# A transposed input made by VectorE from a second, blocked load, in a macaron transformer block

## The reference

```python
x = x + 0.5 * ffn(layernorm(x))        # w = int4-quantised kernel; x @ w + bias + (x @ a) @ b
x = x + attention(layernorm(x))        # 16 heads of 64, keys and values from a latent of 32 columns, causal softmax
x = x + 0.5 * ffn(layernorm(x))        # the same weights again
```

## Time and profile before

| what | value |
|---|---|
| median of 3 executions | 784.86 us (783.91 to 785.38) |
| the profiled execution | 786.69 us, of which the span of instructions is 785.0 us |
| busy: PE, PE weight loads | 757.9 us (97%), 584.5 us (74%) |
| busy: DVE, POOL, ACT | 646.7 us (82%), 648.2 us (83%), 503.2 us (64%) |
| granted TensorE clock, mean | 0.986 |
| DMA | 79.94 MB, 78,933 packets; 15,905 of them under 512 B |

### The profile page before, as it was taken

The page is one execution under the profiler, slowest core; times in us unless marked ns, Lnnn a source line. Parts: engine busy times, 40 slices in busy tenths (PEclk is TensorE's granted clock), DMA queues, the critical chain, the costliest instruction groups (busy, mean ns, idle before and its releaser), DMA issues.

```text
span 785.0 us, 20588 instructions
## 1 busy us (share of the span) xinstructions
PE 757.9 (97%) x7578; PEld 584.5 (74%) x7578; DVE 646.7 (82%) x2044; ACT 503.2 (64%) x979; POOL 648.2 (83%) x449
## 2 busy tenths in 40 slices
PE   8799999999999999999999999999999999999997
PEld 6586677778687777778777877868778776867675
DVE  3788788898889889898988989888888988777635
ACT  6158676667667576666757666675766676665670
POOL 5535778889898888979888898988888897979882
PEclk8799999999999999999999999999999999999999
DMA  4547172644636163553616254362526445260101
GB/s 118 140 101 175 30 175 57 139 109 91 159 75 140 48 144 92 115 134 83 162 42 140 72 133 117 83 166 58 133 59 146 104 98 137 63 159 3 30 2 41
DMA packets 78933, 79.94 MB, mean 102 GB/s; under 512 B 15905, under 2 KB 66353, under 8 KB 78833
## 3 DMA queue, kind: packets, MB, share of 16 engines
q1 hardware_dynamic: 78272, 77.43, 42.5%
q10 hardware_dynamic: 560, 1.20, 0.6%
HBM read 9.91 MB, written 8.39 MB: 23 GB/s over the span
## 4 chain that ended last, share of the span: by engine, by line
PE 84%; DVE 5%; ACT 3%; SPq 3%; issue 2%; DMA 1%; POOL 1%; ACTq 0%; DVEq 0%; POOLq 0%
PE bank L960 17%; PE bank L996 16%; PE bank L924 13%; PE bank L920 8%; PE bank L933 8%; PE bank L1085 7%; PE bank L1040 3%; SPq L420 3%; PE bank L1041 2%; PE bank L1042 2%; PE bank L1031 2%; PE bank L1028 2%; PE bank L1101 1%; DMA q_stack<-max_t 1%; ACT q_stack L725 1%
## 5 line engine op out<-in xcount | busy, mean ns | idle before, releaser
L1246 DVE TENSOR_REDUCE strip_max<-bank 128x8 f32<-128x512 f32 (+1 forms) x384 | 250.3, 683 | 18.5 <-PE bank L996 15.8
L756 ACT ACTIVATE later_probs<-bank 128x512 f32<-128x512 f32 x384 | 217.7, 598 | 56.0 <-PE bank L924 33.4
L621 POOL TENSOR_TENSOR totals<-totals,later_probs 128x1024 f32<-128x1024 f32 x124 | 227.4, 1834 | 12.1 <-POOL totals L621 0.4
L621 POOL TENSOR_TENSOR totals<-first_probs,later_probs 128x1536 f32<-128x1536 f32 x62 | 216.1, 3486 | 13.8 <-ACT later_probs L756 13.8
L756 ACT ACTIVATE first_probs<-bank 128x384 f32<-128x384 f32 (+1 forms) x320 | 153.6, 512 | 109.8 <-PE bank L924 69.3
L996 PE MATMUL bank<-keys,q_stack 118*128 118x512 f32 (+7 forms) x1024 | 208.1, 305 | 1.9 <-DMA q_stack<-q_high 1.1
L996 PEld LDWEIGHTS bank<-keys,q_stack 118*128 118x128 f32 x1024 | 170.2, 190 | 12.7 <-DMA q_stack<-q_high 1.3
L924 PE MATMUL bank<-q_stack,keys 119*128 119x384 f32 (+1 forms) x448 | 176.8, 412 | 1.7 <-ACT first_probs L756 1.0
L1246 DVE TENSOR_REDUCE maxima<-bank 128x1 f32<-128x512 f32 (+1 forms) x192 | 127.6, 679 | 2.6 <-PE bank L996 2.5
L924 PEld LDWEIGHTS bank<-q_stack,keys 119*128 119x128 f32 x448 | 80.8, 188 | 41.7 <-ACT later_probs L756 18.3
L920 PE MATMUL bank<-q_stack,keys 119*128 119x256 f32 x512 | 106.7, 300 | 1.4 <-DMA q_stack<-max_t 0.8
(11 more groups left out here) (152 smaller groups left out, 915.4 us busy)
## 6 DMA issues: line engine op xcount, KB each, us to landing
q_stack<-q_high SPq DMA_DIRECT2D x252, 128.0 KB, 2.4
q_stack<-q_low SPq DMA_DIRECT2D x128, 128.0 KB, 2.4
x_in<-in_L_attn_x_bld_dram SPq DMA_DIRECT2D x16, 256.0 KB, 3.4
out_dram<-x SPq DMA_DIRECT2D x16, 256.0 KB, 3.5
x_back<-out_dram SPq DMA_DIRECT2D x16, 256.0 KB, 3.2
out_dram<-x2b SPq DMA_DIRECT2D x15, 256.0 KB, 2.3
keys<-keys_staged SPq DMA_DIRECT2D x16, 192.0 KB, 2.9
keys<-keys_staged SPq DMA_DIRECT2D x32, 96.0 KB, 2.6
```

The lines of the kernel that those rows point to most:

```text
L621: nc.gpsimd.tensor_tensor(total, first_probs[g % 2][:, :, P:] if j == 1 else total, probs_of(g, j)[:], ALU.add).then_inc(added, 1)
L756: nc.scalar.activation(out, score_bank(t, u)[:, 0:heads * cols].rearrange("p (e q) -> p e q", e=heads), ACT.Exp).then_inc(exp_done, 1)
L1246: nc.vector.tensor_reduce(out, bank[:].rearrange("q (b k) -> q b k", k=strip), AX.X, ALU.max).then_inc(a_free, 1)
```

## The change

The input gets a second way in. `blocks` is a new SBUF tile of 128 partitions by 16 by 32: for each quarter `a` of the partitions, one DMA brings columns `32a` to `32a+31` of all 512 positions, position `32r+q` going to partition `32a+q`, block `r`. One VectorE transpose of 128x512, which turns each 32x32 block by itself, makes `x_t` of it. The transposes of `x_in` on PE (unit 0) and the ACT copy fall away in every round but -2, where they stay under new names (`first_transposes`, `first_copy`). The front has seven units, so all counts on `f_full` and `f_free` drop by one. SP issues the four new DMAs for batch `t+4` behind the maxima of the first half; DVE turns batch `t+3` at place 30 of round `t`. POOL's bias addition to `x_in` waits for the load instead of for unit 0. `wkv4` moves into a tile that is free at the start. The tables of places are new throughout.

```diff
-F_UNITS = 8
+F_UNITS = 7
-KEYS_UNIT, QUERY_UNIT = 3, 4
+KEYS_UNIT, QUERY_UNIT = 2, 3
-FRONT_AT = [2, 4, 11, 15, 19, 30, 31, 37]
+FRONT_AT = [4, 11, 15, 19, 29, 32, 37]
-WEIGH_AT = [[9, 9, 13, 13], [17, 21, 21, 21], [31, 31, 33, 33], [47, 47, 50, 50]]
-ONES_AT = [21, 39, 50, 50]
+WEIGH_AT = [[9, 9, 13, 13], [17, 21, 21, 21], [30, 33, 33, 39], [50, 50, 50, 50]]
+ONES_AT = [17, 39, 46, 50]
-LAST_ONES_AT = [39, 45, 60, 81]
+LAST_ONES_AT = [49, 50, 57, 97]
...
+        blocks = sb("blocks", [P, L // LD, LD])
...
+        def load_blocks(eng, b):
+
+            for a in range(HG):
+                of = x[b][:, a * LD:(a + 1) * LD].rearrange("(r q) c -> q r c", q=LD)
+                eng.dma_start(blocks[a * LD:(a + 1) * LD], of).then_inc(blocks_loaded, DMA)
...
+            load_blocks(sp, 1)
...
                 if attend and top and t > 0:
                     place_max(0)
+                if t + 4 < B:
+                    sp.wait_ge(x_turned, t + 3)
+                    load_blocks(sp, t + 4)
...
                 def add_bias():
-                    wait_batch(pool, f_full, t, 2, F_UNITS, 1)
+                    if is_first(t):
+                        pool.wait_ge(x_full, 1)
+                    else:
+                        wait_batch(pool, x_loaded[par], t, 2, *nth(par))
...
                 def front_copy(n):
                     wait_batch(act, f_full, t, 2, F_UNITS, n + 1)
-                    if n == 0:
-                        nc.scalar.activation(x_t[:], front_bank(t, n)[:], ACT.Copy).then_inc(f_free, 1)
...
                 def front_unit(u):
+                    elif u == 0:
+                        pe.wait_ge(x_turned, t + 2)
...
-                    if u in (0, 2):
-                        if u == 0:
-                            wait_batch(pe, x_loaded[par], t, 2, *nth(par))
+                    if u == 1:
                         for i in range(TT):
-                            if u == 2:
-                                wait_batch(pe, f_normed, t, 2, TT, i + 1)
-                            of = xn[:, i, :] if u else x_in[:, par, i, :]
-                            last = nc.tensor.transpose(bank[:, i * P:(i + 1) * P], of, identity[:])
+                            wait_batch(pe, f_normed, t, 2, TT, i + 1)
+                            last = nc.tensor.transpose(bank[:, i * P:(i + 1) * P], xn[:, i, :], identity[:])
...
+                def turn_input():
+
+                    dve.wait_ge(blocks_loaded, (t + 3) * HG * DMA)
+                    wait_batch(dve, f_full, t, 2, F_UNITS, 1)
+                    nc.vector.transpose(x_t[:], blocks[:].rearrange("q r c -> q (r c)")).then_inc(x_turned, 1)
```

More of the change, by code:

```diff
@@ L151 @@
 OUT_AT = 43
-NEXT_STATS_AT = 23
-TURN_AT = 16
+TURN_INPUT_AT = 30
+NEXT_STATS_AT = 22
+TURN_AT = 17
 INVERT_AT = 7
[L155 to L159, removed]
+SPREAD_AT = [8, 9, 15, 17]
+SCALE_AT = [10, 12, 12, 16]
+ADD_AT = [[8, 10, 10], [17, 17, 23], [26, 29, 38], [49, 50, 50]]
+FIRST_RSTD_AT = 21
 RSTD_AT = 6
[L161 to L179, removed]
+TAIL_RSTD_AT = 37
+BIAS_AT = 4
+TAIL_BIAS_AT = 36
+OPENING_FRONT_AT = [4, 8, 12, 21, 23, 26, 30]
+OPENING_FRONT_ACT_AT = [18, 18, 23, 24, 28, 35, 36]
+OPENING_NORM_AT = [8, 11, 11, 12]
+OPENING_SUM_AT = 6
+OPENING_STATS_AT = 6
+OPENING_LOW_AT = [14, 37, 37, 38, 39, 42]
+OPENING_TURN_AT = 36
+VALUES_AT = 30
+OPENING_TURN_INPUT_AT = 27
+OPENING_NEXT_STATS_AT = 29
+OPENING_FIRST_RSTD_AT = 39
+OPENING_RSTD_AT = 7
+OPENING_BIAS_AT = 3
+LAST_ADD_AT = [[7, 16, 18], [21, 21, 29], [40, 49, 50], [61, 83, 92]]
 AWAKE = 2
@@ L323, in macaron_block @@
         w_chain = sem("w_chain")
+        x_full = sem("x_full")
+        x_free = sem("x_free")
+        blocks_loaded = sem("blocks_loaded")
+        x_turned = sem("x_turned")
         x_loaded = [sem("x_loaded0"), sem("x_loaded1")]
@@ L999, in max_unit, with first_transposes @@
                     last.then_inc(a_full, 1)
+                def first_transposes():
+                    pe.wait_ge(x_loaded[0], DMA)
+                    for i in range(TT):
+                        last = nc.tensor.transpose(aux[:, i * P:(i + 1) * P], x_in[:, 0, i, :], identity[:])
+                    last.then_inc(x_full, 1)
                 def front_unit(u):
                     bank = front_bank(t, u)
-                    if is_first(t) and u == 1:
+                    if is_first(t) and u == 0:
                         centre_weights()
@@ L1127, in one_round @@
                         tail_unit(1 + TAIL_AT.index(u))
+                    if is_first(t) and u == 0:
+                        first_transposes()
                     if prep and u in front_at:
@@ L1139, in one_round @@
                         query_products(0)
[L1140 removed]
+                    if is_first(t) and u == front_at[1]:
                         query_products(1)
@@ L1407, in one_round @@
                         front_stats()
+                    if t + 3 < B and u == turn_input_at:
+                        turn_input()
                     if t + 3 < B and u == next_stats_at:
```

67 lines of the change are left out of this document (36 added, 31 removed).

## The result

| | before | after |
|---|---|---|
| median of 4 runs, us | 784.88 (783.91 to 785.38) | 774.71 (773.26 to 775.53) |
| ratio, 95% interval | | 0.987 (0.9852 to 0.9888) |
| profiled execution, its span, us | 786.69, 785.0 | 775.53, 773.7 |
| a round that nothing disturbs, us | 44.92 | 43.88 |
| rounds 1 to 13 together, us | 586.7 | 573.7 |

What follows compares the result with a forecast made beforehand. PE's stream was taken to bound the kernel. Terms 5.3 + 5.6 + 0.6 - 0.6 = 10.9 us took the span from 785.0 to 774.1 and the median from 784.86 to 774.0; range 770.5 to 782.5.

Steps and rivals of the forecast that it cites:

- What bounds it: Steady round: as long as PE's stream, busy 44.54 of 45.0 us; only what leaves that stream and its waits count.
- The transposes, 14 x 0.38 = 5.3: PE, rounds 0 to 13: four transposes of x_in leave the stream, 0.38 us per round, 5.3 us in all.
- The 390 ns apiece: Rival on PE: the transposes bring their full price; by rows 3.5 us more, 770.5; chance 0.06.
- The covered wait, 5.6: PE before the first query unit, rounds 1 to 13: row sums moved ahead cover the wait for the latents, 5.6 us gained.
- DVE's transpose, 0.65, hidden: DVE, place 30: the added 128x512 transpose takes 0.65 us per batch, hidden by DVE's idle time.
- and 1.3 would be nearly so: DVE, place 30: an added transpose of 1.3 us would still be nearly hidden.
- DVE and SP as rivals: DVE at 5.2 us per transpose, or SP at 1.92 us per issue, loses 21 us: 806; together chance 0.10.
- the margin of 1.1 us at the keys: PE's first max unit, round 4: the last keys land at 245.9, the unit starts at 247.03 without a wait.
- PE waits for keys at the first max unit: Sign that the forecast is wrong: PE's first max unit of a round waits for the keys; no size given.
- The opening, 0.6 gained: Opening after 36.54 us: shorter waits against one more DVE instruction, 0.6 us gained, bounds nothing and 2.5 gained.
- the fifteenth set: Round -1: its removed transposes bring nothing, as PE waits behind them for the query DMA until 36.54 anyway.
- The end, 0.6 lost: Round 16: one more filler block, 0.88 us, less about 0.3 of shortened gap; 0.6 us lost, bounds 0 and 1.5.

Runs made afterwards that it cites:

- e3: The changed kernel with four 128x128 transposes (of the identity) put back on PE ahead of the product with w_ffn in rounds 0 to 15: 778.64 us.
- e5: The changed kernel with ONES_AT[0] at 18 instead of 17, so one score parts the row sums of group 0 from the weighing of group 1: 778.82 us.
- e1: The changed kernel with ONES_AT[0] back from 17 to 21, the row sums of group 0 behind the first query unit again: 782.75 us.
- e12: The changed kernel with the DVE transpose made twice, with a wait of DVE on itself between: 781.41 us.
- e7: The changed kernel with SP's keys DMAs and their waits ahead of the output DMA instead of behind it: 773.71 us.
- e4: The changed kernel with the DVE transpose made three times, each behind a wait for the one before: 793.3 us.
- e11: The changed kernel without the block loads from the third batch on, DVE turning the second batch's blocks each time (output wrong): 773.83 us.
- e13: The changed kernel with ONES_AT[2] alone moved from 46 to 50, its row sums joining those of group 3: 781.21 us.

## Why the prediction was right, and where it was off

- *What bounds it.* PE's stream, right: e3, e5 and e1 each put back a piece of PE's work or of its waiting and the time followed.
- *The transposes, 14 x 0.38 = 5.3.* Right; e3 gives 0.47 at a place next to it. The 390 ns apiece of the Trainium skill ("VectorE: DVE Perf Modes", "The three transpose paths") would make 1.56 per round; no run here shows it.
- *The covered wait, 5.6.* The mechanism was right, with margins of 1.5 us for POOL (1.1 said) and 0.15 for the latents (0.35 said), of which only 0.05 was to spare, since in the kernel before the query unit starts 0.10 behind the end of the transposes. The size was off: I took the idle time of the row for what it costs. It is 0.57 to 0.66 per round (e3, e1), 7.4 to 8.6 us for 13 rounds. This is why a steady round is 43.88 and not 44.2. It is also why the latents' margin was so thin: I set 0.77 of row sums against 0.42 of wait, and the rows of e1 have 0.66 against 0.63. That the wait was covered whole was close to luck.
- *DVE's transpose, 0.65, hidden.* 0.70, hidden, right for the one. The sentence "and 1.3 would be nearly so" failed: e12 shows a margin of 0.3 us. The two reasons, idle time in the round and a wait of 13.8 us at place 28, don't bear it: in the changed kernel that wait is 0.40 a round, as the new order took it up.
- *DVE and SP as rivals.* For DVE, by an estimate from e12, a transpose costs PE from 1.0 us on (0.70 and the 0.3 of e12), and the gain of 1.04 per round would be gone at 2.0, not at 3. For SP, 0.54 apiece was right, but the margin of 1.1 us at the keys was worked out from one round and a median landing. The latest landings left nothing of it even before (8.56 against PE's 8.63), and in the new order, which takes the transposes away ahead of the first max unit, PE comes 0.54 earlier while the keys come when they came. I had named "PE waits for keys at the first max unit" as a sign that the forecast is wrong. It does, in four rounds, for 0.3 to 0.4 us; it cost 1.6 us (e7), and the rest outweighed it.
- *The opening, 0.6 gained.* Up to the first score 0.9 were gained, but the kernel before had its stretch of lower clock there, and the changed kernel has it in round 0. Over both, with the 0.38 that round 0 was to gain, 1.0 was forecast and 0.5 lost. The two max units that now stand before the query unit do shorten its wait (1.75 to 0.76). The wait at the first max unit grew from 1.15 to 3.0, with 0.7 ahead of it gone; of that, 1.3 is only that PE comes earlier (9.5 us behind the query unit, 10.7 before), which costs nothing, as I had said of the fifteenth set, and the rest is that the queries land 0.6 later. That is within chance: in the other traces PE leaves this wait 11.2 to 12.8 us behind the query unit (12.5 here, 11.9 before). For two waits I had no term: PE now waits for ACT ahead of the second and the fourth query unit, 0.71 and 1.57 us. Round 0 is 1.4 longer, with two max units more and the lower clock in it; how it divides stays open. With 78.5 to 79.4 for the same opening in other traces, the 0.5 is no sure loss, but no gain is shown either.
- *The end, 0.6 lost.* Right for the last round, 0.6: the filler came as said, and the gap shrank by more than the 0.3 said (0.96 to 0.43). Round 14 lost another 0.6, where I had looked for nothing. Near its start PE now waits 0.41 for ACT's exponentials, before 0.23; I tested nothing there, and the rest of it is open.

The sum of 10.9 stands against 11.2 in the span. That is nearer than its terms deserve: thirteen steady rounds gave 13.0 where fourteen were to give 10.9, and opening and end took 1.8 where they were to cancel.

## What to carry to other kernels

In this kernel a short wait of PE cost more than the gap that the profile shows: compare the distance between the starts of the neighbours with a place where they follow at once. Idle time of an engine in a round is no cover for what is added to it; the cover is the time between its result and the first one who needs it at that place, and doubling the added instruction measures it in one run. Whoever shortens the stream of the bounding engine ahead of a wait that just didn't show should move what releases that wait as well, and should take the margin there from the latest landing of a DMA over all rounds, not from one round or the median.

## What the runs showed that was not expected

- A PE gap of 0.41 to 0.42 us lengthened the round by 0.57 to 0.66 (e3 against before, e1), one of 0.24 by 0.44 (e12) and one of 0.78 by 1.18 (e4), so 0.15 to 0.4 us beyond the gap.
- One more stretch of 32-column matmuls (twelve row sums set apart from their neighbours) cost 0.36 us of PE, with the same instructions (e5).
- A 128x512 fp32 STREAM_TRANSPOSE from SBUF to SBUF takes 0.70 us; the four of 32x128 from PSUM take 0.31 each.
- A DMA of 64 KB in 512 pieces of 128 bytes is issued in 0.49 us at the median (3.9 at most) and lands 2.4 us later at the median (8.7 at most), as the 128 KB ones of the queries do at the median; the DMA engines' packets went from 78933 to 110613, and without the loads thirteen rounds took 0.6 us less, all of it in the first of them (e11).
- The last keys DMA of a round lands 1.3 us behind the end of its issue in some rounds and 3.1 in others, with the block loads or without them (e11), and it is the late ones that PE feels.
- Over the traces PE ran at the lower clock for 3.4 or for 6.8 us between its query unit and round 1; e13, whose opening is that of the changed kernel, had 6.8 where the changed kernel had 3.4.
